# Delta recurrence: 32-column operands as the loaded weights, results turned back by transposes, state products taken inside the inversion; local layers: residual sum ahead of the row sums

## The reference: what is computed

```
S = S * exp(g_t)
corr = einsum('bhk,bhkv->bhv', k_t, S)
u = (v_t - corr) * b_t
S = S + k_t * u
o_t = einsum('bhk,bhkv->bhv', q_t, S)
```

## Time and profile before

| | |
|---|---|
| median of three runs | 5441.72 us (5439.07 to 5442.9) |
| profiled execution | 5437.88 us |
| its span, first to last instruction | 5435.9 us |
| TensorE busy | 4820.7 us, 89% of the span |
| VectorE, ScalarE, GpSimd busy | 3747.0, 2797.1 and 2115.8 us |
| mean granted TensorE clock | 0.884 |

### The profile page before, as it was taken

One profiled execution on the slowest core, in us unless ns is written; L12 is line 12 of the kernel. 1 busy time (PEld: TensorE's weight loads), 2 busy tenths in 40 slices (PEclk: granted clock), 3 DMA queues, 4 the chain that ended last, 5 costly groups with the idle time before them and its releaser, 6 DMA issues. The chain is left out here.

```text
span 5435.9 us, 193069 instructions
## 1 busy us (share of the span) xinstructions
PE 4820.7 (89%) x82128; PEld 3000.6 (55%) x82128; DVE 3747.0 (69%) x6340; ACT 2797.1 (51%) x5325; POOL 2115.8 (39%) x2244
## 2 busy tenths in 40 slices
PE   5867778686777769999999999999999999999997
PEld 3746657474655735555555555555555555555554
DVE  5454554636455468878788888787877888888774
ACT  4243342424334236666666666666666666666664
POOL 2121121212112135555555555555555555555551
PEclk8676776767676669999999999999999999999999
DMA  0000000000000012222222322233222322232222
GB/s 23 4 3 5 2 5 2 5 4 3 6 2 3 2 59 70 67 61 75 73 68 68 82 72 62 64 79 77 68 62 68 79 68 68 74 78 66 59 62 65
DMA packets 255938, 253.45 MB, mean 47 GB/s; under 512 B 29680, under 2 KB 248816, under 8 KB 254704
## 3 DMA queue, kind: packets, MB, share of 16 engines
q1 hardware_dynamic: 255088, 241.09, 17.6%
HBM read 29.71 MB, written 4.19 MB: 6 GB/s over the span
## 5 line engine op out<-in xcount | busy, mean ns | idle before, releaser
L1468 POOL TENSOR_TENSOR turn<-prod 128x512 f32<-128x512 f32 x768 | 982.2, 1279 | 1393.4 <-DVE prod L1508 1371.1
L1205 PE MATMUL banks<-w2s,xs 128*128 128x512 f32 x2304 | 1185.8, 597 | 37.7 <-DVE xs L1541 30.2
L1508 DVE TENSOR_TENSOR prod<-banks,tabs 128x1024 f32<-128x1024 f32 x768 | 940.1, 1224 | 335.2 <-PE banks L1205 322.2
L1477 POOL TENSOR_TENSOR turn<-turn,rs 128x512 f32<-128x512 f32 x768 | 794.8, 1056 | 285.8 <-ACT rs L1371 285.8
L1239 PEld LDWEIGHTS banks<-msk,turn 128*128 128x128 f32 x3072 | 352.5, 140 | 479.8 <-issue 380.6
L1520 DVE TENSOR_REDUCE ss<-sq 128x8 f32<-128x512 f32 x768 | 493.4, 677 | 11.6 <-ACT sq L1353 9.9
L1353 ACT ACTIVATE sq<-banks 128x512 f32<-128x512 f32 x768 | 456.4, 594 | 54.7 <-DVE prod L1508 20.8
L1239 PE MATMUL banks<-msk,turn 128*128 128x128 f32 x3072 | 471.6, 276 | 4.1 <-ACT qt L1386 2.3
L1287 PE MATMUL banks<-ot,w2s 128*128 128x512 f32 x768 | 430.7, 643 | 34.7 <-DVE y L1581 34.0
L1386 ACT ACTIVATE qt<-banks 128x512 f32<-128x512 f32 x384 | 229.2, 597 | 421.5 <-PE banks L1239 420.7
L1384 ACT ACTIVATE kx<-banks 128x512 f32<-128x512 f32 x384 | 229.3, 597 | 407.6 <-PE banks L1239 407.1
(11 more groups left out here) (217 smaller groups left out, 8398.9 us busy)
## 6 DMA issues: line engine op xcount, KB each, us to landing
v<-v_tok SPq DMA_DIRECT2D x1152, 132.0 KB
v<-v_tok SPq DMA_DIRECT2D x384, 66.0 KB
v<-v SPq DMA_DIRECT2D x188, 132.0 KB, 2.5
w2s<-in_weights SPq DMA_DIRECT2D x10, 768.0 KB, 4.9
tabs<-in_rot SPq DMA_DIRECT2D x40, 128.0 KB, 3.2
w2s<-in_weights SPq DMA_DIRECT2D x1, 2713.5 KB, 11.1
w2s<-in_weights SPq DMA_DIRECT2D x10, 256.0 KB, 3.0
xin<-in_x SPq DMA_DIRECT2D x8, 256.0 KB, 2.8
```

Source lines behind the costliest of these rows:

```text
L1205: pe.matmul(a_bank(use), xs[:, t % 2, b * P:(b + 1) * P], w[:, at:at + 512], start=True, stop=True).then_inc(a_done, 1)
L1468: gp.tensor_tensor(turn[:, r % ROTS, :, :].rearrange(halves, s=2), prod[:, r % 2, 0, :, :].rearrange(halves, s=2), prod[:, r % 2, 1, :, :] ...
L1477: gp.tensor_tensor(turn[:, r % ROTS, :, :], turn[:, r % ROTS, :, :], along(rs[:, q % 2, b, :], DH), ALU.mult).then_inc(rot_done, 1)
L1508: v.tensor_tensor(prod[:, r % 2, :, :, :], a_bank(use).rearrange("p (h d) -> p h d", h=HU).unsqueeze(1) .to_broadcast([P, 2, HU, DH]), tab ...
```

## The change

In the delta layer the four products of the tail with a 32-wide operand change sides: the state, r or u (128 x 32) is now loaded, and the wide matrix moves. The results, 32 partitions a sequence, go to the four 32-partition strips of a bank, one strip a sequence (`at_block(b)`), and come out turned. So each goes through a ScalarE copy to SBUF (`kst`, `ut`, `ost`) and TensorE transposes back. K S and Q S become one product with 256 moving columns (`state_products`), taken inside the inversion, between first and second products of step 1; they are turned back in step 2, and VectorE makes r behind step 3 (`rests`). ScalarE's narrow copies of the next pair's matrix (`take_blocks`) are parted from the wide ones (`take_at`), which go behind the copy of o and K'u. In the local layers `ffn(t, 0)` goes in front of `sums`. The core of the diff:

```diff
+                    def state_products(pair):
+
+                        for x in range(2):
+                            h = 2 * pair + x
+                            if pair:
+                                pe.wait_ge(s_ready, h - 1)
+                            for b in range(NB):
+                                last = pe.matmul(p[3 * x + 1][at_block(b), 0:2 * P], state[:, h, b, :],
+                                                 act_qkv[:, h:h + H1 + 1:H1, b * P:(b + 1) * P],
+                                                 start=True, stop=True, skip_group_check=True)
+                            last.then_inc(ks_ready, 1)
+
+                    def turn_state_products(pair):
+
+                        for x in range(2):
+                            pe.wait_ge(kst_taken, 2 * pair + x + 1)
+                            for i in range(2):
+                                last = pe.transpose(p[3 * x + 1][:, (2 + i) * P:(3 + i) * P], kst[:, x, i, :], ident)
+                            last.then_inc(ks_turned, 1)
+
                     def first_products(pair, i, n):
                         for x in range(2):
                             pe.wait_ge(t_ready, n[x])
                             if i == 1 and pair:
-                                pe.wait_ge(r_ready, 2 * pair - 1 + x)
+                                pe.wait_ge(u_taken, 2 * pair - 1 + x)
                             if i < SMALL:
                                 pe.wait_ge(ao_ready, pair * 2 * (SMALL - 1) + 2 * (i - 1) + x + 1)
...
                         for x in range(2):
                             pe.wait_ge(p1_taken, n[x])
                             if i == 1 and pair:
-                                pe.wait_ge(u_taken, 2 * pair - 1 + x)
-                                pe.wait_ge(s_ready, 2 * pair - 1 + x)
+                                pe.wait_ge(ost_taken, 2 * pair - 1 + x)
...
+                                pe.wait_ge(r_ready, 2 * pair + x + 1)
...
                             first_products(pair, i, n)
+                            if i == 1:
+                                state_products(pair)
+                            elif i == 2:
+                                turn_state_products(pair)
...
                             second_products(pair, i, n)
                         for x, h in enumerate(heads):
-                            for b in range(NB):
-                                s = slice(b * P, (b + 1) * P)
-                                pe.matmul(p[3 * x][:, b * DV:(b + 1) * DV], act_qkv[:, H1 + h, s],
-                                          state[:, h, b, :], start=True, stop=True)
-                                last = pe.matmul(p[3 * x][:, P + b * DV:P + (b + 1) * DV], act_qkv[:, h, s],
-                                                 state[:, h, b, :], start=True, stop=True)
-                            last.then_inc(ks_ready, 1)
-                        if pair + 1 < H1 // 2:
-                            for x in range(2):
-                                turn_a(2 * pair + 2 + x)
-                        for x, h in enumerate(heads):
                             pe.wait_ge(tri_ready, h + 1)
                             pe.wait_ge(lower_spread, h + 1)
                             pe.wait_ge(upper_spread, h + 1)
                             pe.wait_ge(r_ready, h + 1)
                             for b in range(NB):
-                                last = pe.matmul(p[3 * x + 1][:, b * DV:(b + 1) * DV], tt[:, x, b, :],
-                                                 r1[:, x, 2, b, :], start=True, stop=True)
-                            last.then_inc(u_ready, 1)
+                                last = pe.matmul(p[3 * x][at_block(b), 0:P], r1[:, x, 2, b, :], tt[:, x, b, :],
+                                                 start=True, stop=True, skip_group_check=True)
+                            last.then_inc(ut_ready, 1)
+                        if pair + 1 < H1 // 2:
+                            for x in range(2):
+                                turn_a(2 * pair + 2 + x)
+                        for x, h in enumerate(heads):
+                            pe.wait_ge(ut_taken, h + 1)
+                            pe.transpose(p[3 * x][:, P:2 * P], ut[:, x, :], ident).then_inc(u_ready, 1)
                         for x, h in enumerate(heads):
                             pe.wait_ge(u_taken, h + 1)
                             pe.wait_ge(kt_ready, h + 1)
                             pe.wait_ge(pm_ready, h + 1)
                             for b in range(NB):
-                                pe.matmul(p[3 * x + 2][:, b * DV:(b + 1) * DV], pm[:, h % 4, b, :],
-                                          u[:, x, 0, b, :], start=True, stop=True)
-                                last = pe.matmul(p[3 * x + 2][:, P + b * DV:P + (b + 1) * DV], kt[:, x, b, :],
-                                                 u[:, x, 1, b, :], start=True, stop=True)
+                                pe.matmul(p[3 * x + 2][at_block(b), 0:P], u[:, x, 0, b, :], pm[:, h % 4, b, :],
+                                          start=True, stop=True, skip_group_check=True)
+                            for b in range(NB):
+                                last = pe.matmul(p[3 * x + 2][at_block(b), P:2 * P], u[:, x, 1, b, :],
+                                                 kt[:, x, b, :], start=True, stop=True, skip_group_check=True)
+                            last.then_inc(ost_ready, 1)
+                        for x, h in enumerate(heads):
+                            pe.wait_ge(ost_taken, h + 1)
+                            for i in range(2):
+                                last = pe.transpose(p[3 * x + 1][:, i * P:(i + 1) * P], ost[:, x, i, :], ident)
                             last.then_inc(o_ready, 1)
...
-                    def take_at(h):
+                    def take_blocks(h):
                         a.wait_ge(a_turned, h + 1)
...
                         last.then_inc(atc_ready, 1)
-                        a.activation(at[:, x, :, :], blocks(p[6 + x]), ACT.Copy).then_inc(at_ready, 1)
+
+                    def take_at(h):
+                        a.wait_ge(a_turned, h + 1)
+                        a.activation(at[:, h % 2, :, :], blocks(p[6 + h % 2]), ACT.Copy).then_inc(at_ready, 1)
...
+                            if i == 1:
+                                for x in range(2):
+                                    a.wait_ge(ks_ready, 2 * pair + x + 1)
+                                    a.activation(kst[:, x, :, :], blocks(p[3 * x + 1][:, 0:2 * P], 2), ACT.Copy)\
+                                        .then_inc(kst_taken, 1)
...
                                     rstd(NEXT_LN, p[6])
+                        for x in range(2):
+                            a.wait_ge(ut_ready, 2 * pair + x + 1)
+                            a.activation(ut[:, x, :], p[3 * x][:, 0:P], ACT.Copy).then_inc(ut_taken, 1)
+                        if more:
+                            for x in range(2):
+                                take_blocks(2 * pair + 2 + x)
+                        for x in range(2):
+                            a.wait_ge(ost_ready, 2 * pair + x + 1)
+                            a.activation(ost[:, x, :, :], blocks(p[3 * x + 2][:, 0:2 * P], 2), ACT.Copy)\
+                                .then_inc(ost_taken, 1)
                         if more:
...
                         v.transpose(flat_blocks(x, 0), flat_blocks(x, 1)).then_inc(t_ready, 1)
+
+                    def rests(heads):
+
+                        for x, h in enumerate(heads):
+                            v.wait_ge(ks_turned, h + 1)
+                            qs, ks = (blocks(p[3 * x + 1][:, i * P:(i + 1) * P]) for i in (2, 3))
+                            link(v.tensor_tensor(r1[:, x, 0, :, :], ks, along(ex[:, 0, :, h], DV), ALU.mult))
+                            v.tensor_tensor(o2[:, x, :, :], qs, along(ex[:, 0, :, h], DV), ALU.mult)
+                            link(v.tensor_tensor(r1[:, x, 1, :, :], vt[:, :, h * DV:(h + 1) * DV],
+                                                 r1[:, x, 0, :, :], ALU.subtract))
+                            v.tensor_tensor(r1[:, x, 2, :, :], r1[:, x, 1, :, :], along(t24[:, 1, :, h], DV),
+                                            ALU.mult).then_inc(r_ready, 1)
...
+                            if i == 3:
+                                rests(heads)
...
                         for x, h in enumerate(heads):
-                            v.wait_ge(ks_ready, h + 1)
-                            ks, qs = blocks(p[3 * x][:, 0:P]), blocks(p[3 * x][:, P:2 * P])
-                            link(v.tensor_tensor(r1[:, x, 0, :, :], ks, along(ex[:, 0, :, h], DV), ALU.mult))
-                            v.tensor_tensor(o2[:, x, :, :], qs, along(ex[:, 0, :, h], DV), ALU.mult)
-                            link(v.tensor_tensor(r1[:, x, 1, :, :], vt[:, :, h * DV:(h + 1) * DV],
```

(10 more changed lines are left out.)

15 lines of the change are left out of this document (11 added, 4 removed).

## The result

The changed kernel took 5142.84 us (median of 4 runs, 5139.0 to 5148.43) against 5440.93 for the kernel before (median of 4, 5439.07 to 5442.9): a ratio of 0.9453, 95% interval 0.9437 to 0.9469. That is 298 us faster, where 267 were forecast. Its profiled execution is the slowest of the four, with a span of 5146.5 us, 289.4 less than before. One execution of the first experiment's kernel took 15962.74 us in a slow state and stands in none of the ratios.

A forecast was written before the change was run, and what follows sets the result against it. TensorE's 128-column loads were taken to bound the delta layer's tail; 5437.88 less 253 (delta layer) and 20 (local layers) gave 5165 us, put at 5175; own range 5105 to 5230, likeliest at 0.78.

The forecast's parts named there:

- What bounds the kernel: Delta layer, behind each inversion: TensorE's own work sets a 20.57 us tail at clock 0.50, paying for 128-column loads.
- The tail: From the last L455 to the next pair's L405: 8.0 us for 20.57, saving 12.6 us, 16 times.
- the list: Step-by-step schedule of the new tail from the end of L455: 8.65 us at half rate, 6.1 at full.
- Four strips at once: New 128 x 32 products: four strips overlap, so eight passes of 128 columns take about 0.43 us at half rate.
- The inversion's cost: State products in step 1 and transposes in step 2 lengthen each inversion by 1.9 us together.
- the 10 that I put on the sum: Forecast moved from 5165 to 5175 us because L405's overlap was 3.6 of 4 and hops can only be longer.
- The third pair: Tail without turn_a or turn_k: 12.2 us saved less 2.0 in the inversion, 8 times.
- VectorE's rests hidden: Eight operations, 2.3 us, fit in VectorE's idle time before step 4; in the third pair up to 0.8 us shows.
- The local layers: TensorE's wait for the residual sum goes: 20 us saved, bounds 5 and 34.
- Two at a time: Rival: strips overlap two at a time, not four, costing 91 us at half rate; about 5240 us, chance 0.08.
- Pauses for instructions: Rival: TensorE waits for its instructions, one or two pauses an inversion, 60 us; 5235 us, chance 0.07.
- Serial strips: Rival: strips run one after another, 12.7 us a pair at half rate, 305 us; 5480 us, slower, chance 0.04.

The follow-up runs named there:

- the first experiment's kernel: The kernel before with one edit, the residual sum in front of the row sums in the local layers: 5409.93 us, ratio 0.9948.
- ScalarE's old order: The changed kernel with ScalarE's wide copies back with the narrow ones, in front of the ost copies: 5134.98 us, ratio 0.9442.

## Why the prediction was right, and where its sizes were off

- **What bounds the kernel: right.** The tail was TensorE's own work at the price of 128-column loads. In their old form the state products took 6.85 us again inside an inversion. That the load is what is paid, and not the pass as such, stays a reading of rows: loads fill 20.24 of the old tail's 20.60 us and 5.01 of the new one's 7.92; no run varies the loaded columns alone.
- **The tail: right, nearly to the step.** 12.7 and 12.9 us saved by the table, 12.6 forecast. Counted from L535's start (1594.09), the list and the timeline of the last block, in us: u taken 4.4 and 4.26; o and K'u from 3.9 to 5.6 and 3.92 to 5.6; `turn_k` starts 6.95 and 6.84. It then ends at 8.65 on the list and 7.92 here, since the rate rose to full at about 1599.7. That 8.0 lies between the two ends was a choice; the clock rows show the rise that it counted on, not that a denser tail is its reason.
- **Four strips at once: right.** 0.43 us for eight passes at half rate, 0.22 at full, and 0.87 to 0.90 when they may not overlap. L405's 3.6 of 4, for which I moved the forecast up, was no guide for 128-column passes (3.9 of 4); L406 has 3.6 (3.57 / 1.00). The Trainium skill's page "TensorE: Matmul & The Clock Gate", section on packing small matmuls, has 2.38 times for three column tiles that move 512 columns; here, at 128 and 256, the trace gives more per tile, and the measurement decides. The Trainium skill's page "TensorEngine Tiling (Array Packing)", Key Properties, has TensorE drain at a change of mode: L389 (128 x 128) starts at 1595.25, before L535 (128 x 32) is modelled to end at 1595.32, and L430 to L406 likewise. No gap shows, though with modelled ends a short one could hide.
- **The inversion's cost: mechanism right, over-sized.** +1.7, +0.8 and +0.9 us by the table for 1.9, 1.9 and 2.0. The term assumed about as much half rate as before; the tail now ends at full rate, so the second and third inversion of a block begin there and pay 1.0 for L406. Over a block that is 2.4 us too much, 19 us in all, the largest part of the 17 us by which the sum for the profiled execution, 5165, missed its 5148.43 (inversions 19, local layers 8, first two tails 3, less 13 for the third pair). So errors of either sign partly cancelled. The forecast itself was 32 us too high: these 16.6, the 10 that I put on the sum, and 5.6 by which the profiled execution is slower than the median.
- **The third pair: under by 1.6 us.** 10.6 saved for 12.2. Up to the end of the state sums the trace gives 11.7; about 1.1 us come back in the next block's front. Some 0.4 of that is `turn_k`'s wait for the wide copies, which now come after both heads' narrow ones (ScalarE's old order gives 0.5 back there by the table); the rest I have not traced.
- **VectorE's rests hidden: right**, 0.97 us of idle time left behind them, and also in the third pair, where I had up to 0.8 us showing: there at least 0.20 us is left.
- **The local layers: under-sized.** 28 us for 20, and the run of that edit alone gives 28 too. Of the 34 us of wait 28 came off the time; 6 came back elsewhere, where my 20 allowed for 14.
- **Rivals.** Two at a time: excluded by the 0.43. Pauses for instructions: "issue" in front of L430 is 6.8 us in the whole layer (7.4 before) and in front of the second products, L461, 7.2 (4.3 before), far from 60, so no. Serial strips: the mechanism was not there, and its price was wrong by half and more, since I held the clock at 0.50 for them too. That is the step of the prediction that failed by its reasoning: the prices took the rate as given by the place, and with another form of the passes the rate at the same place was another.
- **Slips of the pen.** The low end of my range is 5441.7 - 341 = 5101, not 5105; two at a time would cost 0.85 us a pair for u by my own prices, not 0.4; 267 / 24 is 11.1. None changes a reading.

## What to carry to other kernels

Load the narrow operand and move the wide one, each to its own strip of columns, and turn the result back, when the passes are paced by their loads: here 32 passes of 6.85 us became 16 of 1.0 to 1.9, and turning back cost 0.5 us in step 2 (L416, at full rate). Work that is moved into a busy stretch still costs its full time there; look for the place where the engine already waits (47 us for moving the state products two steps on), and check afterwards which rate the neighbours run at. When a half-rate stretch is re-priced, price both forms at both rates: here a rival's price was wrong by half because the rate was another with the other form.

## What the runs showed of the hardware

- TensorE's granted clock fell from 1.00 to 0.50 with no idle time at all, into a run of passes that load 128 columns and move 32: after 0.9 to 1.5 us in 12 tails of 16, after 3.4 to 7.7 us in four. The changed kernel's tails, with passes that move 128 columns over 32-column loads, begin at 0.50 and all end at 1.00.
- Work without use made the kernel faster: 2.4 us of filler in a wait of 2.5 us brought 22 us, with full rate in the 64 x 64 products (2.5 us for 3.3) and a tail shorter by 1.0 to 1.5 us.
- Four 128 x 32 strips ran 3.9 products at once at 128 columns each (0.87 us serial, 0.22 in four strips, both at clock 1.00), 3.6 at 256 (3.57 and 1.00 us).
